# Local attention layers: PE takes value products two and two together, and the transposes between them in one run

## The reference

```python
xn = _layernorm(x, axis=-1)
s = _L0_attn_ref(xn, L0_attn_w_qkv, L0_attn_w_out)      # global attention, 16 heads of 16, rope
g = _silu(_L0_ffn_ref(xn, ...))                         # two local layers
x = x + s * g
# one local layer:
h = shift_token(x)
q, k, v = split(h @ wqkv)                               # 8 heads of 64
q = l2norm(q) * qs;  k = l2norm(k) * ksc
q, k = rotary_xpos(q, k)
sim = einsum('bhwid,bhwjd->bhwij', bq, bk)              # a window of 128 against itself and the window before
attn = softmax(where(mask, -max, sim))
o = einsum('bhwij,bhwjd->bhwid', attn, bv)
x = x + o @ wo
h = layernorm(shift_token(x)) * lg + lb
a, g = split(h @ w1 + b1)
x = x + (a * gelu(g)) @ w2 + b2
```

## Time and profile before

| | |
|---|---|
| median of three executions | 2620.13 us |
| lowest and highest | 2616.96 and 2620.86 us |
| span of the profiled execution, first to last instruction | 2620.8 us |
| PE busy | 2449.0 us, 93% |
| DVE busy | 1634.4 us, 62% |
| ACT busy | 1424.8 us, 54% |
| POOL busy | 674.8 us, 26% |

### The profile page before, as it was taken

How to read it: one execution, slowest core, us unless ns; L and a number is a source line. 1 busy time by engine, 2 the same in 40 slices (tenths; PEclk the granted TensorE clock), 3 DMA queues, 4 the chain that set the end, 5 groups by cost and what they waited for, 6 DMA issues and landing times. The chain is left out here.

```text
span 2620.8 us, 40347 instructions
## 1 busy us (share of the span) xinstructions
PE 2449.0 (93%) x12576; PEld 1537.8 (59%) x12576; DVE 1634.4 (62%) x3713; ACT 1424.8 (54%) x2634; POOL 674.8 (26%) x548
## 2 busy tenths in 40 slices
PE   7937999999999997989999999999989999999978
PEld 4513454455554544766766776676666676677543
DVE  6646888888888883665564655555465465555426
ACT  2203666666666665755655655565565565556421
POOL 4411211111011002543332333233333333233000
PEclk9957999999999998999999999999999999999989
DMA  4546122122121201000000000000100000000006
GB/s 144 193 132 190 53 62 64 46 67 61 50 64 55 59 30 43 1 1 1 1 0 0 0 0 0 24 1 8 32 1 1 1 0 0 0 0 0 1 8 198
DMA packets 72020, 104.21 MB, mean 40 GB/s; under 512 B 11965, under 2 KB 47249, under 8 KB 71825
## 3 DMA queue, kind: packets, MB, share of 16 engines
q1 hardware_dynamic: 71936, 103.16, 12.8%
HBM read 69.06 MB, written 39.49 MB: 41 GB/s over the span
## 5 line engine op out<-in xcount | busy, mean ns | idle before, releaser
L666 DVE TENSOR_REDUCE maxima<-ps_m 128x1 f32<-128x512 f32 x1024 | 646.4, 685 | 188.9 <-PE ps_m L560 185.7
L737 ACT ACTIVATE probs<-ps_st 128x1024 f32<-128x1024 f32 x512 | 498.6, 1022 | 260.2 <-PE ps_st L592 260.1
L560 PE MATMUL ps_m<-k_st,q_st 96*128 96x512 f32 x1024 | 400.9, 443 | 37.2 <-DMA k_st<-ks 29.0
L560 PEld LDWEIGHTS ps_m<-k_st,q_st 96*128 96x128 f32 x1024 | 178.9, 193 | 291.4 <-DVE maxima L666 233.5
L592 PE MATMUL ps_st<-q_st,k_st 96*128 96x512 f32 x1024 | 319.7, 400 | 1.1 <-ACT max_rows L720 0.4
L1255 ACT ACTIVATE l_probs<-l_probs,l_neg_max 128x256 f32<-128x256 f32 x512 | 254.4, 499 | 71.0 <-DVE l_neg_max L1384 68.3
L604 PE MATMUL ps_o<-probs,v_st 128*32 128x512 f32 x2048 | 272.7, 605 | 0.6 <-ACT probs L737 0.6
L1234 ACT COPY p_turned<-ring 128x512 f32<-128x512 f32 x256 | 144.4, 592 | 227.4 <-PE ring L1049 227.4
L1384 DVE CUSTOM_DVE_ANT_1 l_probs<-ring,l_mask 128x256 f32<-128x256 f32 x384 | 145.3, 422 | 131.3 <-PE ring L1086 125.1
L592 PEld LDWEIGHTS ps_st<-q_st,k_st 96*128 96x128 f32 x1024 | 189.3, 189 | 63.8 <-issue 13.0
L1009 POOL TENSOR_SCALAR clipped<-sumsq 128x16 f32<-128x16 f32 x64 | 16.1, 251 | 808.4 <-DVE sumsq L1361 808.4
(11 more groups left out here) (153 smaller groups left out, 3942.3 us busy)
## 6 DMA issues: line engine op xcount, KB each, us to landing
q_st<-qs SPq DMA_DIRECT2D x64, 256.0 KB
k_st<-ks SPq DMA_DIRECT2D x128, 128.0 KB
qs<-split SPq DMA_DIRECT2D x16, 512.0 KB, 3.5
ks<-split SPq DMA_DIRECT2D x16, 512.0 KB, 5.1
o<-o_sb SPq DMA_DIRECT2D x32, 256.0 KB, 13.1
x_in<-in_L_attn_x_dram SPq DMA_DIRECT2D x8, 512.0 KB, 5.9
v<-v_sb SPq DMA_DIRECT2D x16, 256.0 KB, 4.7
v_in<-v SPq DMA_DIRECT2D x8, 512.0 KB, 4.1
```

Source lines behind the costliest of these rows:

```text
L560: nc.tensor.matmul(bank(base, use)[:, :], q_st[u][j][:, qt * P:(qt + 1) * P], k_st[u][j][:, h * CH:(h + 1) * CH], start=True, stop=True).t ...
L666: nc.vector.tensor_reduce(maxima[:, par, e // 2 % 2, tile + e // 4, e % 2:e % 2 + 1], bank(base, k + e)[:, :], AX_X, ALU.max).then_inc(m_u ...
L737: nc.scalar.activation(probs[:, kt % 4, j, :], ps_st[j][:, :], ACT.Exp, scale=float(G_DIM) ** -0.5).then_inc(exp_done, 1)
```

## The change

In PE's body of the local layers the calls between the second run of transposed probabilities and the scores change places. Before they are: values 0, probabilities 2, values 1, probabilities 3, queries, values 2, keys, values 3. After: values 0 and 1, probabilities 2 and 3, queries, keys, values 2 and 3. No call is added or dropped, and the order of ACT, DVE, POOL and SP is as before.

```diff
--- before.py
+++ after.py
@@ -1155,16 +1155,14 @@
                             hidden_tile(g, lf, 4)
                         if old:
                             values(W, w, 0)
+                            values(W, w, 1)
                             turn_probs(W, 2)
-                            values(W, w, 1)
                             turn_probs(W, 3)
                         if mid_:
                             turn_qk(W, 0)
+                            turn_qk(W, 1)
                         if old:
                             values(W, w, 2)
-                        if mid_:
-                            turn_qk(W, 1)
-                        if old:
                             values(W, w, 3)
                         if forward and w == 0:
                             mean(g)
```

## The result

The changed kernel took 2623.49 us (median of 20 runs, 2621.49 to 2626.55), the kernel before 2619.81 us (20 runs, 2615.73 to 2621.95) beside it. The ratio is 1.0015 with a 95% interval of 1.0008 to 1.0021, so +3.7 us (2.1 to 5.5). The forecast was 2620.5 us in a range of 2613 to 2632, and no difference beyond 0.2%: both hold. The difference is nevertheless a real one, and the forecast's +0.4 is too small by some 3 us; the range of 19 us was wide enough to hold that. One of twelve later executions of the changed kernel (experiment 8) took 3096 us and is left out of the ratio there.

The account below looks back on a forecast made before the run. PE's own order was taken to bound the kernel, busy 2449 of 2620.8 us. Terms of -3.0 (43 windows with other work), +3.6 (18 without) and -0.2 (last window) gave +0.4: 2620.5 us, range 2613 to 2632.

Parts of the forecast that it names:

- A change of kind costs 0.155 us: On PE, each switch between value products and transposes costs 0.155 us; four fewer switches save 0.62 us a window without waits.
- V costs 0.43 behind V: On PE, a value run directly behind another value run costs 0.43 us, where a lone run takes 0.58 to 0.59.
- Rival 1: A second joined value run on PE costs its full 0.59 us, so joining values saves nothing: 2636 us, chance 0.12.
- Rival 2: A second joined value run on PE costs only 0.33 us, its column halves overlapping: 2612 us, chance 0.08.
- New waits take the gain back: Query and key transposes wait for ACT's copies of probabilities 2 and 3; the waits take 0.55 of 0.62 us a window.
- Rival 3: All four switches of kind on PE are saved and the new waits for ACT don't show: 2593 us, chance 0.03.
- Next work at V0 + 4.47: In 43 windows with other PE work, following work starts 4.47 us behind value run 0, before 4.54: -3.0 us together.
- S at V0 + 5.02 in windows without other work: Scores start 5.02 us behind value run 0, before 4.82, held by ACT's chain: +0.20 in 18 windows, +3.6 us.
- The last window takes 0.2 less: The last window, which has no query and key transposes, gets 0.2 us shorter.
- rival 4: PE's clock falls because joined transposes have waits of about half a microsecond among them: 2790 us, chance 0.02.
- POOL may overwrite `qk_n` 0.5 us earlier: Key transposes finish 0.5 us earlier in a window, freeing POOL's write; nobody waits for it then, so counted as nothing.
- Two later waits for DVE cover a later S: In two of 20 windows without other work, later PE waits for DVE of 5.73 and 3.55 us hide later scores.

Follow-up runs that it names:

- experiment 8: The changed kernel and the kernel before, both unaltered, timed and profiled once more: 2623.62 us (1.0011) and 2619.42 us (0.9996).
- experiment 1: Kernel before with only the front half of the change, value runs 0 and 1 joined: 2630.74 us, 1.0038 of before.
- Experiment 2: Kernel before with only the second half of the change, keys right behind queries and value runs 2 and 3 joined: 2628.09 us, 1.0035 of before.
- experiment 3: Kernel before with four buffers for turned probabilities and all four value runs joined, transposes in pairs or all together: 2581.07 us, 0.9847 of before.
- experiment 5: ACT's copies of transposed probabilities halved, in both orders: changed order 2605.78 us (0.9939 of before), old order 2615.36 us (0.9981).
- experiment 7: Kernel before with the changed order only in windows where PE has no other work: 2624.15 us, 1.0012 of before.

## Why the prediction held, and which term was small

- *A change of kind costs 0.155 us, V costs 0.43 behind V.* Shown by experiment 1 and by the changed kernel: 1.02 to 1.03 for two value runs, as for two transpose runs. Rival 1 (0.59) would have given 1.18. Rival 2 (0.33) falls by the same row. The Trainium skill's rule ("TensorEngine Tiling (Array Packing)", Key Properties), that a change of tile within a mode doesn't drain, was borne out by it.
- *New waits take the gain back.* Shown by experiments 2, 3 and 5. TQ was forecast at V0 + 2.37 and came at 2.36. Rival 3 (no waits) would have had TQ at T2 + 0.97 at most, which is what two transpose runs and a change of kind take in experiment 3 (1729.62 - 1728.65); it came at T2 + 1.33.
- *Next work at V0 + 4.47, -0.07 a window.* Here the size was off: 4.53, so -0.02. The pair TQ and TK took 1753.46 - 1752.32 = 1.14, where the working had 0.49 + 0.59 = 1.08. I had put 0.06 us from the end of a copy to PE, read from V0. For TQ at w = 2 it is 0.05. For TK it is more: the second of ACT's two copies (1751.68 + 1.08) ended at 1752.76 and TK started at 1752.91, so 0.14 passed, and it was 0.14 to 0.15 in all 63 windows. Experiment 2 shows TK alone, at 1755.58: its copy ran from 1754.85 and took 0.58, the same again. That makes the stretch some 0.05 longer than forecast, and over 43 windows this is the 2.2 us that are missing (-3.0 forecast, -0.7 and -0.9 found in 38 of them, -0.1 in four more). Why one wait ends in 0.05 and the other in 0.14 stays open. In the early windows TQ shows the longer one too:

```profile
1127.26 1.10 PE L1049 MATMUL ring<-l_ident,l_probs 128*128 128x128 f32 x8
1128.69 1.11 PE L1073 MATMUL ring<-l_ident,qk_n 128*128 128x128 f32 x8 [0.33 <-ACT p_turned L1232]
...
1131.24 1.10 PE L1086 MATMUL ring<-k_ring,q_pad 128*128 128x256 f32 x4 [0.41 <-ACT k_ring L1246]
```

  There TQ is at T2 + 1.43, and S at V0 + 5.06.
- *S at V0 + 5.02 in windows without other work, +0.20 each.* 4.98 and 5.06 were found. The sum, 18 x 0.20 = +3.6, was +3.3, and experiment 7 shows it alone at +3.1 (0.3 to 5.8).
- *The last window takes 0.2 less.* It gave nothing: the next work came 5.57 us behind T0 before and 5.56 in the second profile of the changed kernel, as PE waits there for DVE (`f_low`) in both, 0.48 and 0.64 us. Joined runs end earlier and the wait takes it up.
- *Clock (rival 4).* The steady windows stay at 1.00; their pitches leave no room for a spell at the lower level. The first profile of the changed kernel has one among the joined runs of the last window, 0.51 from 2464.3 to 2467.8, and the next work came 6.22 behind T0 instead of 5.56; the second profile has none there. Behind the long waits the clock falls in some profiles of either order, as window 41 shows. The Trainium skill's rule that the full clock doesn't engage for transposes ("TensorE: Matmul & The Clock Gate", PE-mode transpose) isn't borne out: runs of sixteen transposes stand here at 1.00.
- *POOL may overwrite `qk_n` 0.5 us earlier and "has no one waiting for it then".* This term was put at nothing without its neighbour: nobody waits for POOL's result, but DVE is held up by POOL's instruction. What it costs depends on the clock. With the clock at 1.00 ahead of TK it cost nothing in window 41, since `qk_n` stood beside the second scaling in either order. With the clock fallen there the window was 1.6 us longer in the new order (23.0 against 21.4), in one profile, that of experiment 7, against three of the old; its clock also fell some 0.4 us later, so that the order alone makes the difference isn't shown. How often either comes in the timed executions no run tells.
- *What makes 3.7 us.* The steady windows give +2.3 to +2.6, where the sum had +0.4: some 2 us of the difference are TK's later start, 0.2 the last window, and the term of the scores was 0.3 too large. The 1.1 to 1.4 us that are left are no more than the measurement's interval allows. Windows 31 and 41 could hold them; that isn't shown.
- *Two later waits for DVE cover a later S.* Right for the first: S came at V0 + 5.04 there and the wait shrank from 5.73 to 5.48 us. Right for the second too where the clock was 1.00 (window 41): the wait shrank from 3.55 to 3.31.

## What to carry to other kernels

Joining runs of one kind on PE saves its changes of kind (0.155 us each here), but a run must not come to stand right behind the one whose bank it takes over: reckon the copy that clears the bank from the start of the run that fills it (0.70 + 0.59 + 0.05 to 0.15 us), and put something of the other kind that long between. When an order gains nothing, ask for the missing buffer: the same eight runs, in an order that two more buffers of probabilities allow, were worth some 40 us, and the buffers alone nothing that could be told from zero. And before a difference of some microseconds is explained, take a second profile of the kernel before.

## What the runs showed that I had not expected

- A float32 operation of DVE on SBUF operands and one of POOL held each other up: 3.45 against 5.15 us for two scalings, 0.99 against 2.58 for two `tensor_scalar`, with one more `qk_n` (1.9 us) beside them. The other way round `qk_n` took 3.98 beside DVE's casts and subtractions, which kept their 0.75 and 1.28.
- A fall of the clock behind the same 2.82 us wait comes in some executions and not in others, and here the window with the fall was 4.3 us shorter: POOL and DVE stayed apart (1.7), and no stretch at the lower level came behind the later wait (the rest).
- Two profiles of one kernel differ by 3.8 us in span with every steady window equal to 0.02 us.
